# Vision block on one core: the side work between the attention groups in another order

## The chip, the cores and the metric

One core of a Trainium2 chip runs the whole program; the other cores are idle. The metric is the device time of one execution in microseconds (us), as the median of several runs. In the trace PE is TensorE (PEld its weight loads), DVE VectorE, ACT ScalarE, POOL GpSimd, and SP the SyncE, whose only work here is to issue DMAs.

## The reference

```python
x = x + window_attention(layernorm(x))      # x: (16, 56, 56, 32) f32; 7x7 windows shifted by 3, 4 heads of 8
t = x as 16 x 3136 tokens of 32 channels
t = t + moe(layernorm(t))                   # 8 experts of 32x32, each token uses its best 2

# window attention, per window of 49 tokens and head
attn = softmax((q * 8**-0.5) @ k.T)         # no bias inside the softmax
attn = attn + bias[head] + mask[window]     # relative bias and the shift mask are added after it
out  = (attn @ v) joined over heads @ w_proj + b_proj
# moe
p = softmax(x @ router_w + router_b); top 2, renormalised; out = sum of p_k * (x @ expert_w[k] + expert_b[k])
```

## The kernel before

The image batch is cut into 16 units. A unit is one half, 28 columns, of two images: 64 windows, four side by side in the partitions and 16 along. Each unit goes through four phases, and the program is a software pipeline over them: in one step of the main loop the attention of unit u is computed, and between its pieces stand small side tasks of its neighbours. These are the preparation of unit u+1 (`keep`, `xt`, `qk`, `place`, `kmask`, `v`, `ob`), loading and the first layernorm of unit u+2 (`load`, `norm1_*`), projection, second layernorm and router of unit u-1 (`ot`, `y`, `back`, `norm2_*`, `x2t`, `router`, `top2`, `replicate`), and the expert products of unit u-2 (`wt`, `mix`, `mix_drain`, `final`, `store`).

The attention of a unit is four groups g = 0 to 3, of 16 windows each. A group is a chain over all engines, and every link works on the same four PSUM banks `ps_win`: PE writes the unshifted scores (`maximum`, L1232), DVE takes their largest (L907) and splits its negative in two bf16 parts (`ms`, L921 and L923), PE turns these (`shift`, L1240), ACT copies them (`mr`, L801), PE writes the scores again with the shift (`scores`, L1255 and L1261), ACT takes the exponentials (L810), and PE multiplies with the values (`pv`, L1276) while the next `maximum` has to wait until the exponentials have read the banks. I call the DVE maximum of group g `mx0` to `mx3`; the preparation of a unit's own group 0 is done in the step before, so a step runs from one `mx0` to the next.

The side tasks stand in a table, `SIDE_TASKS`, keyed (g, slot): slot 0 after the scores of group g, slot 1 after the next `maximum`, slot 2 after `pv`, slot 3 after `shift`. One function, `macro_step`, walks it in order, and every engine runs through the same list and takes out only what is its own. So the table fixes the order on each engine, and a task moved past tasks of other engines only changes nothing. Engines meet by semaphores. Nothing is scheduled by a planner.

The tasks that matter here, and their engines:

- `top2` 4 (DVE, L1002 to L1004) makes the two probabilities; `top2` 5 to 7 (POOL, L661 to L677, seven instructions in a chain) make the weights in three bf16 parts; `wt` turns them (PE, L1337) and copies them (ACT, L827); each `mix` i spreads them over the partitions in the one bank `ps_weight` (PE, L1348) and DVE multiplies (L1022). With one bank, `mix` i+1 on PE waits for DVE's product of `mix` i.
- `ot` 0 and 1 turn the attention output (PE, L1290) and copy it (ACT, L789); `y` 0 and 1 project it (PE, L1300); `back` 0 and 1 add the input (DVE, L948); `norm2_center` sums (DVE, L897) and subtracts the mean (POOL, L608 and L612).
- `keep` (POOL, L602) copies the loaded input of the next unit; it waits for `back` 1 of the unit two before, whose buffer it takes.
- `final` 0 and 1 turn the expert sum back (PE, L1307) and add (DVE, L1031, `xo`); `ob` 0 and 1 are the bias part of the attention output (PE, L1214).
- `load`, `replicate` and `store` are issued by SP alone; `kmask` is ACT's (L756), `place` POOL's (L636).

Short products share two banks, `ps_shared` and `ps_acc`; `ON_ACC` says which use the second. `bank_free` makes each fill wait for the drain of the one that was in the same bank before it. After the last unit the tasks that remain are interleaved by the counts in `TAIL`.

Of the kernel before, what the change touches and what calls it, by code (L numbers as in the profile page):

```python
# [69 lines left out]
PRE_ORDER = ("keep", "xt", "qk", "place", "kmask", "v", "ob")  # L70
LATE = ("wt", "mix", "mix_drain", "final", "store")
SIDE_TASKS = {
    (0, 0): [("ot", 1), ("keep", 0), ("wt", 0), ("load", 0), ("y", 0), ("mix", 0), ("back", 0), ("mix", 1), ("y", 1), ("back", 1), ("norm2_center", 0), ("xt", 0), ("mix", 2)],
    (0, 1): [("xt", 1), ("mix", 3)],
    (0, 2): [],
    (0, 3): [("norm2_square", 0), ("qk", 0), ("mix", 4)],
    (1, 0): [("mix", 5), ("norm2_scale", 0), ("norm1_center", 0), ("qk", 1), ("mix", 6), ("kmask", 0)],
    (1, 1): [("mix", 7), ("qk", 2)],
    (1, 2): [],
    (1, 3): [("mix", 8)],  # L80
    (2, 0): [("mix", 9), ("mix_drain", 0), ("mix", 10), ("place", 0), ("x2t", 0), ("mix", 11)],
# [1354 lines left out]
```

## Time and profile before

| | us |
|---|---|
| median of 3 runs | 802.82 (799.15 to 818.51) |
| profiled execution, device time | 804.47 |
| its span, first to last instruction | 802.7 |
| mean granted TensorE clock | 0.946 of full speed |
| one step of the main loop at full clock, `mx0` to `mx0` | 44.0 to 44.6 |
| PE / DVE / POOL / ACT busy | 83% / 69% / 64% / 49% |

The device time is 1.8 us above the span. The profiled run lies 1.65 us above the median. The rows below give the start and the duration in us, the engine, the line, the operation, what it writes and reads, and in brackets the idle time before it with what ended it. Durations of PE rows are modelled and overlap a little with the next row. A row of busy time by stretch has the stretch, its length, the busy us (and instructions) of PE, PEld, DVE, ACT and POOL, the granted clock, the DMA share and GB/s; where it is for one line, only that engine's.

### The profile page before, as it was taken

What the parts mean: (1) busy time and instruction counts of PE and PEld (TensorE: products, weight loads), DVE (VectorE), ACT (ScalarE), POOL (GpSimd) and SP (SyncE); (2) the same over time, 40 slices, a digit from 0 to 9 for tenths busy, and PEclk for the clock granted to TensorE, in tenths of its full rate; (3) what the DMA queues carried; (4) which work ended last, traced back from release to release, by engine and by line L of the source; (5) the groups of instructions that cost most, each with busy time, mean ns of one, the idle gap of its engine ahead of it and who ended that gap; (6) DMA issues with size and microseconds to landing.
All of it is one profiled execution on the core that took longest, in us unless ns stands there. A gap on an engine that the chain in (4) does not pass through costs nothing.

```text
span 802.7 us, 29444 instructions
## 1 busy us (share of the span) xinstructions
PE 665.8 (83%) x12602; PEld 439.5 (55%) x12632; DVE 553.3 (69%) x1003; ACT 395.0 (49%) x641; POOL 515.8 (64%) x555
## 2 busy tenths in 40 slices
PE   0678789989798898989898988989898988987775
PEld 0446565656556565656556565656556565655431
DVE  7433567868686868868686667868576777756634
ACT  1555464546474565555463654555464564533100
POOL 4745685859677776859586676859577776442620
PEclk9987998999999999999999899999899999989759
DMA  2000030312304041313113040313203040303140
GB/s 72 21 23 2 22 82 22 84 42 49 69 25 87 24 99 25 84 42 81 44 40 75 13 103 22 83 43 72 52 20 86 22 100 5 83 22 72 31 101 20
DMA packets 16962, 41.48 MB, mean 52 GB/s; under 512 B 9281, under 2 KB 9409, under 8 KB 15297
## 3 DMA queue, kind: packets, MB, share of 16 engines
q1 hardware_dynamic: 16240, 38.59, 21.6%
q8 instruction: 100, 1.64, 0.9%
q10 hardware_dynamic: 592, 1.01, 0.4%
q14 instruction: 30, 0.24, 0.1%
HBM read 7.47 MB, written 6.42 MB: 17 GB/s over the span
## 4 chain that ended last, share of the span: by engine, by line
PE 43%; DVE 36%; issue 8%; POOL 7%; ACT 4%; SPq 0%; DMA 0%; DVEq 0%; POOLq 0%; ACTq 0%
DVE mx L907 9%; PE ps_win L1261 5%; PE ps_weight L1348 4%; PE ps_pv L1276 4%; PE ps_acc L1368 4%; PE ps_win L1232 4%; DVE ms L921 4%; DVE zt L1022 3%; PE ps_shared L1187 3%; DVE x L1022 3%; PE ps_shared L1300 2%; PE ps_win L1255 2%; PE ps_win L1240 2%; DVE ms L923 2%; PE ps_acc L1187 2%
## 5 line engine op out<-in xcount | busy, mean ns | idle before, releaser
L907 DVE TENSOR_REDUCE mx<-ps_win 128x32 f32<-128x1568 f32 x64 | 114.3, 1786 | 36.7 <-PE ps_win L1232 36.7
L1022 DVE TENSOR_TENSOR zt<-ps_weight,x 128x392 f32<-128x392 f32 x118 | 66.1, 561 | 100.3 <-PE ps_weight L1348 100.3
L1276 PEld LDWEIGHTS ps_pv<-vb,pt 128*49 128x49 f32 x4096 | 101.2, 128 | 25.6 <-issue 25.3
L810 ACT ACTIVATE pt<-ps_win 128x1568 f32<-128x1568 f32 x64 | 94.6, 1478 | 41.7 <-PE ps_win L1261 40.3
L1276 PE MATMUL ps_pv<-vb,pt 128*49 128x18 f32 x4096 | 107.4, 200 | 0.0
L1348 PE MATMUL ps_weight<-wt,const_bf_tile 96*128 96x392 bf16 x234 | 81.5, 348 | 20.8 <-DVE zt L1022 19.2
L644 POOL TENSOR_TENSOR on<-on,obs 128x256 f32<-128x256 f32 x64 | 46.6, 729 | 79.0 <-DVE on L934 79.0
L1022 DVE TENSOR_TENSOR x<-ps_weight,x 128x392 f32<-128x392 f32 x116 | 65.3, 563 | 28.7 <-PE ps_weight L1348 27.2
L602 POOL TENSOR_TENSOR x_kept<-xin,weight_tile 112x896 f32<-112x896 f32 x16 | 33.9, 2120 | 68.6 <-DVE x L948 68.6
L590 POOL TENSOR_TENSOR st<-st,minus_half 112x28 f32<-112x28 f32 x16 | 77.0, 4810 | 1.2
L623 POOL TENSOR_TENSOR st<-st,minus_half 112x28 f32<-112x28 f32 x16 | 76.9, 4806 | 1.2
L801 ACT COPY mr<-ps_win 128x512 bf16<-128x512 bf16 x64 | 37.5, 586 | 78.6 <-PE ps_win L1240 76.6
L636 POOL TENSOR_SCALAR qbd<-qp,const_tile 128x392 f32<-128x392 f32 x128 | 75.5, 601 | 0.0
L1261 PE MATMUL ps_win<-qbd,kp 32*49 32x196 f32 x2048 | 74.4, 349 | 0.0
L756 ACT ACTIVATE kbd<-kp,const_tile 128x392 f32<-128x392 f32 x128 | 69.3, 617 | 0.5
L1348 PEld LDWEIGHTS ps_weight<-wt,const_bf_tile 96*128 96x128 bf16 x234 | 23.0, 98 | 80.6 <-DVE zt L1022 39.7
L1232 PE MATMUL ps_win<-kbd,qp 32*49 32x196 f32 x2048 | 60.2, 344 | 5.4 <-ACT pt L810 4.2
L768 ACT COPY vb<-ps_shared 49x512 f32<-49x512 f32 x62 | 36.8, 593 | 40.5 <-PE ps_shared L1198 40.2
L1232 PEld LDWEIGHTS ps_win<-kbd,qp 32*49 32x49 f32 x2048 | 35.2, 122 | 24.9 <-issue 17.4
L1187 PE MATMUL ps_shared<-xt,weight_tile 128*128 128x392 f32 x94 | 44.1, 552 | 0.6 <-ACT xt L734 0.6
L1240 PE MATMUL ps_win<-const_bf_tile,ms 128*128 128x128 bf16 x256 | 26.5, 229 | 21.8 <-DVE ms L923 21.2
L1255 PE MATMUL ps_win<-mr,const_bf_tile 32*49 32x196 bf16 x1024 | 37.1, 267 | 7.2 <-ACT mr L801 7.2
(161 smaller groups left out, 1351.1 us busy)
## 6 DMA issues: line engine op xcount, KB each, us to landing
x<-x SPq DMA_DIRECT2D x48, 392.0 KB, 5.1
x<-x2t SPq DMA_DIRECT2D x64, 98.0 KB, 2.2
xin<-x SPq DMA_DIRECT2D x32, 150.0 KB
out<-xo SPq DMA_DIRECT2D x32, 150.0 KB
xin<-x SPq DMA_DIRECT2D x32, 18.0 KB
out<-xo SPq DMA_DIRECT2D x30, 18.0 KB
xin<-x SPq DMA_DIRECT2D x32, 15.6 KB
xin<-x SPq DMA_DIRECT2D x32, 1.9 KB
```

What stands on the lines that cost most here:

```text
L590: nc.gpsimd.tensor_tensor(st1[:, 4, :], st1[:, 3, :], minus_half[:, :], ALU.pow).then_inc(rstd1, 1)
L623: nc.gpsimd.tensor_tensor(st2[:, 4, :], st2[:, 3, :], minus_half[:, :], ALU.pow).then_inc(rstd2, 1)
L636: nc.gpsimd.tensor_scalar(qbd[i][:, :, h, :], qp[v.par][:, 8 * i:8 * i + 8, :], head_rows[:, h:h + 1], 1.0, ALU.mult, ALU.mult).then_inc(q ...
L756: ins = nc.scalar.activation(kbd[i][:, :, h, :], kp[v.par][:, 8 * i:8 * i + 8, :], ACT.Copy, scale=head_rows[:, h:h + 1])
L810: nc.scalar.activation(pt[g % 2].rearrange("p a x h n -> p a (x h n)"), ps_win[:, :, 0:2 * HN], ACT.Exp).then_inc(probs_ready, 1)
L907: nc.vector.tensor_reduce(mx[g % 2].rearrange("n a x h -> n a (x h)"), ps_win[:, :, 0:8 * N].rearrange("n a (k m) -> n a k m", m=N), AX, A ...
L1022: nc.vector.tensor_tensor(tokens if eh else zt[:, a, :], weight_bank(w, 1 + i)[:, 0:HALF], tokens, ALU.mult).then_inc(weight_drained, 1)
L1187: mm(pre_bank(v, 2 + i)[:, 0:HALF], (wk if i % 2 else wq)[:, :], xt[:, 8 * b:8 * b + 8, :, :].rearrange("p q k i -> p (q k i)"), start=Tru ...
L1232: ins = mm(ps_win[PAD * k:PAD * k + N, a, HN * x:HN * x + HN], qp[u.par][r, q, :], kbd[g // 2][r, q % 8, :, :].rearrange("p h n -> p (h n) ...
L1261: ins = mm(ps_win[PAD * k:PAD * k + N, a, HN * x:HN * x + HN], kp[u.par][r, q, :], qbd[g // 2][r, q % 8, :, :].rearrange("p h n -> p (h n) ...
L1276: ins = mm(ps_pv[PAD * x:PAD * x + N, c0:c0 + SLOT], pt[g % 2][:, a, x, h, :], vb[u.par][:, 2 * g + x, a, h, :], start=True, stop=True)
L1348: mm(weight_bank(w, 1 + i)[:, 0:HALF], weight_sel[:, eh, a, :], wt[:, HALF * half:HALF * half + HALF], start=True, stop=True).then_inc(wei ...
```

## The change

Only the table changes, and one entry of `ON_ACC`. No instruction is added or removed. Two lines of the table and the set:

```diff
-    (0, 0): [("ot", 1), ("keep", 0), ("wt", 0), ("load", 0), ("y", 0), ("mix", 0), ("back", 0), ("mix", 1), ("y", 1), ("back", 1), ("norm2_center", 0), ("xt", 0), ("mix", 2)],
+    (0, 0): [("ot", 1), ("wt", 0), ("keep", 0), ("y", 0), ("back", 0), ("mix", 0), ("y", 1), ("back", 1), ("mix", 1), ("xt", 0), ("norm2_center", 0), ("mix", 2)],
...
-    (3, 2): [("top2", 4), ("mix_drain", 1), ("ob", 0), ("final", 0), ("top2", 5)],
-    (3, 3): [("ot", 0), ("final", 1), ("top2", 6), ("store", 0), ("top2", 7), ("ob", 1)],
+    (3, 2): [("mix_drain", 1)],
+    (3, 3): [("replicate", 0), ("final", 0), ("ob", 0), ("top2", 4), ("top2", 5), ("top2", 6), ("ob", 1), ("final", 1), ("store", 0), ("top2", 7), ("ot", 0)],
...
-ON_ACC = {("ot", 1), ("xt", 1), ("qk", 0), ("y", 1), ("ot", 0), ("ob", 0), ("router", 0), ("x2t", 1)}
+ON_ACC = {("xt", 1), ("qk", 0), ("y", 1), ("ot", 0), ("ob", 0), ("router", 0), ("x2t", 1)}
```

The other moves: `load` from (0, 0) to (0, 3) and `replicate` from (3, 0) to (3, 3); `qk` 1 and `kmask` 0 to the front of (1, 0), with `norm2_scale` ahead of `mix` 5; `place` 0 from (2, 0) to (1, 1); `norm1_square` and `norm1_scale` from (2, 2) and (2, 3) to (2, 1); `place` 1 from (3, 1) to (2, 3); `top2_exp` from (3, 0) to (3, 1).

What becomes of this on PE, from the `pv` of group 3 on (L1276), is this order before:

```order
L1276 MATMUL ps_pv<-vb,pt 49x18 x32
L1214 MATMUL ps_acc<-vb,bt 64x16x16
L1214 MATMUL ps_acc<-vb,bt 64x2x4x16 x2
L1214 MATMUL ps_acc<-vb,bt 64x16x16
L1214 MATMUL ps_acc<-vb,bt 64x2x4x16 x2
L1307 MATMUL ps_weight<-const_tile,ym 112x128 x4
L1240 MATMUL ps_win<-const_bf_tile,ms 128x128 x4
L1290 MATMUL ps_acc<-const_tile,on 128x2x64 x4
L1307 MATMUL ps_weight<-const_tile,ym 112x128 x3
L1214 MATMUL ps_shared<-vb,bt 64x16x16
L1214 MATMUL ps_shared<-vb,bt 64x2x4x16 x2
L1214 MATMUL ps_shared<-vb,bt 64x16x16
```

and this now:

```order
L1276 MATMUL ps_pv<-vb,pt 49x18 x32
L1240 MATMUL ps_win<-const_bf_tile,ms 128x128 x4
L1307 MATMUL ps_weight<-const_tile,ym 112x128 x4
L1214 MATMUL ps_acc<-vb,bt 64x16x16
L1214 MATMUL ps_acc<-vb,bt 64x2x4x16 x2
L1214 MATMUL ps_acc<-vb,bt 64x16x16
L1214 MATMUL ps_acc<-vb,bt 64x2x4x16 x2
L1214 MATMUL ps_shared<-vb,bt 64x16x16
L1214 MATMUL ps_shared<-vb,bt 64x2x4x16 x2
L1214 MATMUL ps_shared<-vb,bt 64x16x16
L1214 MATMUL ps_shared<-vb,bt 64x2x4x16 x2
L1307 MATMUL ps_weight<-const_tile,ym 112x128 x3
```

The turn of the shift (L1240) moves ahead of the first `ob` (the L1214 rows into `ps_acc`) and of `final` 0 (the first L1307), both `ob` stand together, and `ot` 0 (L1290) comes behind `final` 1, as the next row after these twelve.

On DVE, from the normalisation of group 3 (L930, L934) to the sum of the second layernorm (L897), before:

```order
L930 RECIPROCAL rz<-ps_pv 128x32
L934 TENSOR_TENSOR on<-ps_pv,rz 128x16x2x8
L1002 TENSOR_SCALAR top<-top 112x28
L1003 RECIPROCAL top<-top 112x28
L1004 TENSOR_TENSOR top<-top 112x28
L1031 TENSOR_TENSOR xo<-ps_weight,x_1 112x4x4x32
L1031 TENSOR_TENSOR xo<-ps_weight,x_1 112x3x4x32
L1022 TENSOR_TENSOR zt<-ps_weight,x_0 128x392
L948 TENSOR_TENSOR x_1<-ps_shared,x_kept 112x4x4x32
L1022 TENSOR_TENSOR zt<-ps_weight,x_0 128x392
L948 TENSOR_TENSOR x_1<-ps_acc,x_kept 112x3x4x32
L897 TENSOR_REDUCE st<-x_1 112x28
```

and now:

```order
L930 RECIPROCAL rz<-ps_pv 128x32
L934 TENSOR_TENSOR on<-ps_pv,rz 128x16x2x8
L1031 TENSOR_TENSOR xo<-ps_weight,x_1 112x4x4x32
L1002 TENSOR_SCALAR top<-top 112x28
L1003 RECIPROCAL top<-top 112x28
L1004 TENSOR_TENSOR top<-top 112x28
L1031 TENSOR_TENSOR xo<-ps_weight,x_1 112x3x4x32
L948 TENSOR_TENSOR x_1<-ps_shared,x_kept 112x4x4x32
L1022 TENSOR_TENSOR zt<-ps_weight,x_0 128x392
L948 TENSOR_TENSOR x_1<-ps_acc,x_kept 112x3x4x32
L1022 TENSOR_TENSOR zt<-ps_weight,x_0 128x392
L897 TENSOR_REDUCE st<-x_1 112x28
```

`xo` of `final` 0 (L1031) moves ahead of the three instructions of `top2` 4 (L1002 to L1004), and each `back` (L948) ahead of the product (L1022) that stood before it.

On PE in the slot (0, 0), from `ot` 1 (L1290) to `mix` 2 (the last L1348), before:

```order
L1290 MATMUL ps_acc<-const_tile,on 128x2x64 x4
L1337 MATMUL ps_weight<-const_bf_tile,w_parts 96x112 x7
L1300 MATMUL ps_shared<-weight_tile,ot 112x128 x4
L1348 MATMUL ps_weight<-wt,const_bf_tile 128x392 x2
L1300 MATMUL ps_acc<-weight_tile,ot 112x128 x3
L1179 MATMUL ps_shared<-const_tile,xc 128x112 x4
L1348 MATMUL ps_weight<-wt,const_bf_tile 128x392
```

and now:

```order
L1290 MATMUL ps_shared<-const_tile,on 128x2x64 x4
L1337 MATMUL ps_weight<-const_bf_tile,w_parts 96x112 x7
L1300 MATMUL ps_shared<-weight_tile,ot 112x128 x4
L1348 MATMUL ps_weight<-wt,const_bf_tile 128x392
L1300 MATMUL ps_acc<-weight_tile,ot 112x128 x3
L1348 MATMUL ps_weight<-wt,const_bf_tile 128x392
L1179 MATMUL ps_shared<-const_tile,xc 128x112 x4
L1348 MATMUL ps_weight<-wt,const_bf_tile 128x392
```

`mix` 1 (the second L1348) moves behind `y` 1 (the second L1300), and `ot` 1 writes the other bank.

On SP every instruction keeps its place.

## Rows read from the trace of the kernel before

**Rows 1.** The page: the chain that ended last, by engine.

```profile
PE 43%; DVE 36%; issue 8%; POOL 7%; ACT 4%; SPq 0%; DMA 0%; DVEq 0%; POOLq 0%; ACTq 0%
```

**Rows 2.** Busy time by stretch: a full step, and its part mx0 to mx1.

```profile
377.51:421.50 43.99, 38.76 (x776) 25.85 (x779) 33.74 (x62) 24.68 (x40) 32.15 (x35) 1.00 0.26 57
421.50:437.60 16.10, 13.96 (x266) 10.76 (x265) 9.92 (x20) 7.46 (x14) 10.37 (x15) 1.00 0.36 78
```

**Rows 3.** Timeline of DVE, steps of units 9 and 10, mx0 to mx1.

```profile
426.37 0.37 DVE L1004 TENSOR_TENSOR top<-top 112x28 f32<-112x28 f32 x1
...
426.78 0.69 DVE L1031 TENSOR_TENSOR xo<-ps_weight,x 112x512 f32<-112x512 f32 x1
...
434.35 0.68 DVE L948 TENSOR_TENSOR x<-ps_shared,x_kept 112x512 f32<-112x512 f32 x1
...
435.53 0.56 DVE L948 TENSOR_TENSOR x<-ps_acc,x_kept 112x384 f32<-112x384 f32 x1
...
437.60 1.78 DVE L907 TENSOR_REDUCE mx<-ps_win 128x32 f32<-128x1568 f32 x1
...
439.41 1.08 DVE L921 TENSOR_SCALAR ms<-mx 128x32 bf16<-128x32 f32 x1
```

**Rows 4.** Timeline of POOL, the same stretch.

```profile
426.82 0.57 POOL L661 TENSOR_TENSOR pick<-pick,top 112x224 f32<-112x224 f32 x1
...
430.98 0.61 POOL L677 TENSOR_TENSOR w_parts<-mix_rest,w_parts 112x224 bf16<-112x224 f32 x1
...
436.26 2.12 POOL L602 TENSOR_TENSOR x_kept<-xin,weight_tile 112x896 f32<-112x896 f32 x1 [4.67 <-DVE x L948]
...
438.65 1.74 POOL L612 TENSOR_TENSOR xc<-x,st 112x896 f32<-112x896 f32 x1
```

**Rows 5.** Timeline of PE, the same stretch.

```profile
426.40 0.39 PE L1240 MATMUL ps_win<-const_bf_tile,ms 128*128 128x128 bf16 x4
...
427.61 0.51 PE L1307 MATMUL ps_weight<-const_tile,ym 128*112 128x128 f32 x3 [0.24 <-DVE xo L1031]
...
429.31 0.29 PE L1255 MATMUL ps_win<-mr,const_bf_tile 32*49 32x196 bf16 x8
...
431.73 0.52 PE L1337 MATMUL ps_weight<-const_bf_tile,w_parts 112*96 112x112 bf16 x7 [0.65 <-POOL w_parts L677]
...
432.57 1.10 PE L1300 MATMUL ps_shared<-weight_tile,ot 128*112 128x128 f32 x8 [0.32 <-ACT ot L789]
...
433.50 0.33 PE L1348 MATMUL ps_weight<-wt,const_bf_tile 96*128 96x392 bf16 x1
...
440.88 0.61 PE L1240 MATMUL ps_win<-const_bf_tile,ms 128*128 128x128 bf16 x4 [1.23 <-DVE ms L923]
```

**Rows 6.** Timeline of ACT, the same stretch.

```profile
432.30 0.81 ACT L827 COPY wt<-ps_weight 96x784 bf16<-96x784 bf16 x1
```

**Rows 7.** Busy time of L921 alone after mx1, of two units.

```profile
172.00:177.00 5.00, 1.08 (x1) 1.00 0.28 76
710.60:715.60 5.00, 0.24 (x1) 0.75 0.01 3
```

**Rows 8.** Timeline of POOL and of DVE, after mx2 of unit 8.

```profile
401.65 4.80 POOL L623 TENSOR_TENSOR st<-st,minus_half 112x28 f32<-112x28 f32 x1
...
404.43 0.24 DVE L921 TENSOR_SCALAR ms<-mx 128x32 bf16<-128x32 f32 x1
```

**Rows 9.** Busy time by stretch, mx1 to mx2 of units 8, 9 and 10.

```profile
393.39:402.60 9.21, 7.85 (x168) 4.59 (x169) 7.83 (x12) 4.66 (x7) 4.88 (x7) 1.00 0.18 45
437.60:449.48 11.88, 10.51 (x168) 5.46 (x169) 7.92 (x12) 4.75 (x7) 5.52 (x7) 0.71 0.15 37
484.47:495.20 10.73, 9.36 (x168) 5.22 (x169) 7.83 (x12) 4.74 (x7) 4.88 (x7) 0.84 0.15 39
```

**Rows 10.** Timeline of PE after the last unit's attention.

```profile
744.87 0.86 PE L1307 MATMUL ps_weight<-const_tile,ym 128*112 128x128 f32 x3 [0.75 <-DVE xo L1031]
```

**Rows 11.** Timeline of ACT, the same place.

```profile
744.16 0.51 ACT L789 COPY ot<-ps_acc 128x392 f32<-128x392 f32 x1 [3.71 <-PE ps_acc L1290]
```

More of the change, by code:

```diff
@@ L72 @@
 SIDE_TASKS = {
-    (0, 0): [("ot", 1), ("keep", 0), ("wt", 0), ("load", 0), ("y", 0), ("mix", 0), ("back", 0), ("mix", 1), ("y", 1), ("back", 1), ("norm2_center", 0), ("xt", 0), ("mix", 2)],
+    (0, 0): [("ot", 1), ("wt", 0), ("keep", 0), ("y", 0), ("back", 0), ("mix", 0), ("y", 1), ("back", 1), ("mix", 1), ("xt", 0), ("norm2_center", 0), ("mix", 2)],
     (0, 1): [("xt", 1), ("mix", 3)],
     (0, 2): [],
-    (0, 3): [("norm2_square", 0), ("qk", 0), ("mix", 4)],
-    (1, 0): [("mix", 5), ("norm2_scale", 0), ("norm1_center", 0), ("qk", 1), ("mix", 6), ("kmask", 0)],
-    (1, 1): [("mix", 7), ("qk", 2)],
+    (0, 3): [("norm2_square", 0), ("load", 0), ("qk", 0), ("mix", 4)],
+    (1, 0): [("qk", 1), ("kmask", 0), ("norm2_scale", 0), ("mix", 5), ("norm1_center", 0), ("mix", 6)],
+    (1, 1): [("mix", 7), ("qk", 2), ("place", 0)],
     (1, 2): [],
     (1, 3): [("mix", 8)],
-    (2, 0): [("mix", 9), ("mix_drain", 0), ("mix", 10), ("place", 0), ("x2t", 0), ("mix", 11)],
[7 rows of a table removed]
+    (2, 0): [("mix", 9), ("mix_drain", 0), ("mix", 10), ("x2t", 0), ("mix", 11)],
+    (2, 1): [("norm1_square", 0), ("norm1_scale", 0)],
+    (2, 2): [("qk", 3), ("x2t", 1), ("mix", 12)],
+    (2, 3): [("router", 0), ("place", 1), ("kmask", 1), ("top2", 0)],
+    (3, 0): [("mix", 13), ("top2", 1), ("mix", 14), ("top2", 2), ("v", 0), ("mix", 15)],
+    (3, 1): [("top2_exp", 0), ("top2", 3), ("v", 1), ("mix", 16)],
+    (3, 2): [("mix_drain", 1)],
+    (3, 3): [("replicate", 0), ("final", 0), ("ob", 0), ("top2", 4), ("top2", 5), ("top2", 6), ("ob", 1), ("final", 1), ("store", 0), ("top2", 7), ("ot", 0)],
 }
```

5 rows, old and new, of the table SIDE_TASKS are left out of this document.

## The prediction

> **What bounds the kernel now.** I read the page first: no engine is busy for more than 83% of the span, and in the chain that ended last PE has 43% and DVE 36% [rows 1]. So nothing is bound by throughput over the whole; the end is set by a chain that hops between PE and DVE, and what counts is which wait ends last at each hop. Next the stretches: a step at full clock takes 43.99 us, and 16.10 of it lie between mx0 and mx1, where PE is busy 13.96 and DVE 9.92 [rows 2]. The other three parts of a step share the remaining 27.9 us, with the same attention work in each, so mx0 to mx1 is where side work costs most. There I read the timelines of all engines side by side.
>
> Three things are to be seen in it. First, PE is nearly without a gap from `pv` of group 3 until the scores of the next unit's group 0 at 429.31; its one gap is 0.24 us before `final` 1 [rows 5]. Second, after these scores PE waits 0.65 us until POOL has the last of the weight parts (`wt`), then 0.32 us for ACT's copy of `ot` before `y` 0 at 432.57 [rows 5]. Third, mx1 starts at 437.60 and ends at 439.38, but L921 behind it takes 1.08 us and ends at 440.49, and PE waits 1.23 us for it before it turns the shift at 440.88 [rows 3, 5]. Another L921 took 0.24 us [rows 8]. Its end is 0.10 us behind the end of POOL's L612 at 438.65 + 1.74 = 440.39 [rows 4]: DVE has to wait for that POOL instruction. The unit of 172 us has the same 1.08 us, and so have all of units 3 to 14 (1.07 or 1.08, once 1.38); the last unit, which has no `keep` and so an earlier L612, has 0.24 [rows 7]. So the last link before PE in group 1 is not DVE's own work but POOL's chain `back` 1, `keep`, L608, L612.
>
> **Edits that cost nothing.** SP issues `load`, `replicate` and `store` in the same sequence with the same waits, so moving `load` and `replicate` does nothing at all. `kmask` 0 follows `qk` 1 on ACT as before, with `mix` (which is not ACT's) gone from between them; `top2_exp` stays between `v` 0 and `v` 1 on ACT. `wt` and `keep` share no engine. On POOL, `place` 0 (about 2.5 us) now stands before the addition of group 1 and `norm1_scale` (about 7 us) before that of group 2. Who waits for these additions is `ot` 0, some 10 us on; they stay covered. The sum L891 now stands ahead of DVE's normalisation of group 2, 1.07 us, in a run of DVE work whose sum is unchanged, and the square it needs is two us old. `qk` 1 ahead of `mix` 5 leaves PE's sum between scores and maximum unchanged. `norm2_scale` starts about 1.3 us earlier, and its reader `x2t` was not waiting. If that cover were gone, each would cost at most its own length in a step, and I see no such case.
>
> **The turn of the shift ahead of `ob` and `final` 0.** In place of 426.40, PE turns as soon as `pv` is done and the shift is ready, before the 1.3 us of `ob` 0 and most of `final` 0. But the scores stand behind the same PE work (`ob` 0, `ob` 1, `final` 0 and 1, `ot` 0), so they gain only the gap of 0.24 us [rows 5]. That lets `ot` 1 end earlier, and there the next wait takes it all.
>
> **`xo` ahead of `top2` 4.** This is the step that costs. DVE's `xo` takes 0.69 us, and L1004 ended just before it [rows 3]. So L1004 ends 0.69 us later, POOL's chain starts at 427.51 in place of 426.82 and ends at 432.28 in place of 430.98 + 0.61 = 431.59 [rows 4]. PE's `wt` goes from 431.73 to 432.42, ends at 432.94, and `y` 0 follows: 432.57 becomes 432.94, 0.37 later (before, `y` 0 waited for `ot` a further 0.32, which swallows the rest) [rows 5]. ACT's copy goes from 432.30 to 432.99 and ends at 433.80 [rows 6], so `mix` 0 starts at 433.85 in place of 433.50 [rows 5].
>
> **`back` ahead of `mix`.** This gives it back and more. `back` 0 started at 434.35 because it stood behind the product of `mix` 0. Now it starts when `y` 0 is full, 432.94 + 1.10 + 0.05 = 434.09. Then 0.60 for it and 0.48 for the product (start to start): `back` 1 at 435.17 in place of 435.53, 0.36 earlier [rows 3]. `y` 1 is ready by then, since it no longer stands behind `mix` 1. `keep` and L612 follow `back` 1 directly, so L612 ends at 440.03 in place of 440.39 [rows 4], L921 at 440.13, and PE turns at 440.52 in place of 440.88. On DVE itself mx1 comes about 0.1 us later, at 437.7, and ends at 439.5; it has 0.6 us left before it becomes the later of the two. So the step gains 0.36 us, and in groups 1 to 3 nothing behind it changes. Twelve steps, those of units 3 to 14, show the stretched L921: 12 x 0.36 = 4.3 us.
>
> The bounds of this term: at best L921 meets POOL idle and takes 0.24 [rows 7], 0.84 us less, 10 us in all. At worst the early `back` is eaten and the 0.35 us of `mix` 0 reaches mx1 and everything after it, a loss of 4 us in all. I take 4.3 since both ends of it are worked from neighbouring rows of one stretch.
>
> The Trainium skill, page "SBUF — State Buffer", section "Who interferes with whom", says that DVE and GpSimd share a pair of ports as an exclusive lock, held for the whole instruction. L612 and L921 agree with it. The pow of POOL does not: it ran from 401.65 to 406.45, and an L921 inside it at 404.43 took 0.24 us [rows 8]. If the rule held there too, mx2 would already pay some 2 us a step, and an earlier pow would give a part of it back; the row says that there is nothing to give.
>
> **The tail.** `final` 1 now stands before both `ot`, and `ot` 1 of the last unit waits until ACT has copied `ot` 0, 0.51 us [rows 11], where before `final` 1 and its wait of 0.75 us lay between the two [rows 10]. That wait stays, so `ot` 1 comes 0.7 us later on the path. Start-up: nothing.
>
> **Sum.** 804.47 - 4.3 + 0.7 = 800.9 us for the profiled execution, which lies 1.65 above the median: **799 us**, 0.995 of before. A difference under 2% (16 us) is about what a measurement of this kernel cannot tell from none; the three runs of before span more than that.
>
> **Rivals.**
>
> *The falls of the clock go away.* Between mx1 and mx2 unit 8 took 9.21 us at clock 1.00, unit 9 11.88 at 0.71, unit 10 10.73 at 0.84 [rows 9]; units 12 and 13 repeat the pair. Each time the clock fell to 1.2 GHz around the turn of the shift, after the wait of 1.23 us; in the other units the same wait passed without one, so it stands close to the edge. Together 2.7 + 1.5 + 2.8 + 1.5 = 8.5 us. A wait shortened by 0.36 could be on the right side: 799 - 8.5 = 790.5, and 785 with the best end of the term. For it: the wait becomes shorter. Against it: the wait before `wt` becomes longer.
>
> The Trainium skill, page "TensorE: Matmul & The Clock Gate", section "What's actually happening", lets the clock fall by lack of recent activity. The rows agree in kind; what they don't show is how short a wait is short enough.
>
> *The falls multiply: the slower one.* After the scores PE waits 0.65 us for POOL before `wt` now; by the sum above 432.42 - 431.1 = 1.3 us, the longest wait of the step. If it makes the clock fall in each of the twelve steps, at 2.7 us each, in place of the four falls: 32 - 8.5 = 24, or 823 us. It takes two more long falls to use up the gain, and eight to pass 2%. Against it: `wt` and `ot` waits together were 0.97 us before, with no fall there in any unit.
>
> *The gain is eaten.* POOL's chain comes still later, or L612 meets another DVE instruction, and half a microsecond more is lost before `y` 0: 801 to 806. This is also the case that the reordering does nothing on the path.
>
> **Chances.** Forecast (795 to 801) 0.45; falls gone (785 to 794) 0.24; eaten 0.18; falls multiply (806 to 823) 0.13. Half of the second lies beyond 2% faster (under 786.8) with the best end of the term and a few lost falls at the start of the run: 0.13. More than half of the last lies beyond 818.9: 0.08. The range of 8 in 10 leaves out a tenth on each side: 786 to 812.
>
> **What the profile of the changed kernel would show.** L921 after mx1 still above 0.24 us and ending with L612; the turn behind it some 0.4 us earlier after mx0; PE's wait before `wt` at 1.3 us in place of 0.65; `back` 1 ahead of the product of `mix` 1; 43.6 us a step at full clock; `mr` of group 0 over a microsecond earlier without earlier scores. The forecast is wrong if the wait before `wt` exceeds 1.8 us, if a new wait appears on POOL's additions of groups 1 and 2, or if the clock falls in other places or another number than four of the steps.

## The result, and the profile after

The changed kernel takes 831.7 us (median; 826.3 to 838.5), the kernel before 806.3 us in the same comparison. The ratio is 1.036, with a 95% interval of 1.032 to 1.040: clearly slower, where 799 us was forecast. The profiled execution has a span of 828.0 us, 25.3 more than before. Some executions are slow ones with a lower clock: all ratios leave them out, the medians do not, and the profiled executions of e5 and e10 below are of that kind and are read only where the clock is full.

The page barely moves. First the granted clock in 40 slices of the span, in tenths of full speed, then the chain by engine, which answers to [rows 1]:

```profile
PEclk9989999999998989999998989999999999998766
...
PE 42%; DVE 37%; POOL 8%; issue 7%; ACT 5%; DVEq 0%; POOLq 0%; ACTq 0%
```

DVE, POOL and ACT have each a point more of the chain, PE and issue one less. The stretches say where the time went. These are the four parts of one step at full clock (stretch, its us, busy us of PE, PEld, DVE, ACT, POOL, granted clock, DMA share, GB/s):

```profile
392.56:407.89 15.33, 12.21 (x225) 9.39 (x226) 9.17 (x19) 7.10 (x13) 7.37 (x11) 1.00 0.20 46
407.89:416.71 8.82, 8.00 (x171) 4.72 (x170) 7.62 (x12) 5.85 (x9) 5.77 (x7) 1.00 0.19 47
416.71:424.72 8.01, 7.34 (x175) 4.38 (x175) 5.59 (x11) 4.97 (x8) 7.85 (x8) 1.00 0.02 5
424.72:438.12 13.40, 10.77 (x214) 7.58 (x212) 12.44 (x21) 6.58 (x12) 11.27 (x12) 1.00 0.43 92
```

The first part, mx0 to mx1, takes 15.33 us, against 16.10 in [rows 2] and 15.9 in the undisturbed steps; the second takes 8.82 against 9.21 [rows 9]. Both are shorter, as forecast. The last one, mx3 to mx0, takes 13.40 us where it took 10.9 before, and DVE is busy 12.44 us of it with the same 21 instructions as before. That is 2.5 us a step, in the steps of units 2 to 13: 30 us.

Here is the inside of that part: DVE's second run of `top2`, what POOL did meanwhile, and PE behind it.

```profile
433.63 0.38 DVE L969 TENSOR_REDUCE top<-logits 112x28 f32<-112x224 f32 x1
...
434.04 2.37 DVE L970 TENSOR_TENSOR tmp<-logits,top 112x224 f32<-112x224 f32 x1
...
436.45 0.67 DVE L971 TENSOR_TENSOR tmp<-tmp,const_tile 112x224 f32<-112x224 f32 x1
...
437.15 0.46 DVE L996 TENSOR_TENSOR top<-top 112x28 f32<-112x28 f32 x1
...
433.64 1.70 POOL L594 TENSOR_TENSOR xc<-xc,st 112x896 f32<-112x896 f32 x1
...
435.30 0.73 POOL L644 TENSOR_TENSOR on<-on,obs 128x256 f32<-128x256 f32 x1
...
435.98 0.18 POOL L634 TENSOR_TENSOR turn<-minus_half 1x1 f32<-1x1 f32 x1
...
436.16 2.56 POOL L636 TENSOR_SCALAR qbd<-qp,const_tile 128x392 f32<-128x392 f32 x4
...
438.26 0.87 PE L1368 MATMUL ps_acc<-x,weight_tile 128*32 128x392 f32 x8 [1.69 <-DVE x L1022]
...
439.06 2.37 PE L1276 MATMUL ps_pv<-vb,pt 128*49 128x18 f32 x64
```

L970 compares 224 columns and should take 0.39 us. It starts at 434.04 and ends at 436.41. POOL's L594, the scaling at the end of `norm1_scale`, runs from 433.64 to 435.34, and the addition L644 of group 2 follows it without a gap to 436.03; from there to L970's end are 0.38 us, its plain duration. So L970 took as long as if DVE did nothing until both POOL instructions were over, and its own work after that. L971 and L996 are stretched too, to 0.67 and 0.46 us from 0.39 and 0.19, while `place` 1 (L636) runs. DVE shows no idle time: the wait is hidden inside the duration of an instruction. PE then waits 1.69 us for the product behind it, and the `pv` that follows takes 2.37 us in place of the 1.65 us of the other groups: the granted clock fell to 1.2 GHz in it.

Of all executions of that line in the span (min, median, max in ns):

```profile
L970 DVE TENSOR_TENSOR tmp<-logits,top x32: 391/392/2394, 105.5 to 795.4; 112x224 f32<-112x224 f32 x32
```

Before, no L970 took more than 0.41 us. There the last DVE instruction of `top2` in this place, L996, had ended at 420.98 when L594 began:

```profile
420.79 0.19 DVE L996 TENSOR_TENSOR top<-top 112x28 f32<-112x28 f32 x1
...
421.24 1.70 POOL L594 TENSOR_TENSOR xc<-xc,st 112x896 f32<-112x896 f32 x1
```

The two missed each other by 0.26 us here, and by 0.25 to 0.27 us in ten of the twelve steps. In unit 12 it was 0.08 us, and in unit 9 L594 began 0.08 us before L996 was over, without harm. L594 then ran under mx0, a reduction out of PSUM, which took its usual 1.78 us. That was 10.63 us after mx3; now L594 begins 8.92 us after it, since the sum L891, which POOL's chain waits for, starts 2.23 us after mx3 in place of 3.94.

The rest of the profile answers to [rows 3, 5, 10]: PE before `wt`, `y` 0, the turn of group 1 and the last unit's `ot` 1; DVE's `back` 1 and L921 of group 1.

```profile
402.87 0.52 PE L1337 MATMUL ps_weight<-const_bf_tile,w_parts 112*96 112x112 bf16 x7 [2.42 <-POOL w_parts L677]
...
403.23 1.09 PE L1300 MATMUL ps_shared<-weight_tile,ot 128*112 128x128 f32 x8
...
410.77 0.40 PE L1240 MATMUL ps_win<-const_bf_tile,ms 128*128 128x128 bf16 x4 [0.82 <-DVE ms L923]
...
768.77 1.12 PE L1290 MATMUL ps_shared<-const_tile,on 128*128 128x128 f32 x4 [0.60 <-ACT ot L789]
...
405.43 0.55 DVE L948 TENSOR_TENSOR x<-ps_acc,x_kept 112x384 f32<-112x384 f32 x1
...
409.71 0.68 DVE L921 TENSOR_SCALAR ms<-mx 128x32 bf16<-128x32 f32 x1
```

L921 of group 1 takes 0.68 us in place of 1.08, and the turn behind it waits 0.82 us in place of 1.23. The wait before `wt` is 2.42 us in this unit; in units 5, 6, 9 and 10, where PE comes late because its clock is low, it is 0.2 us or less.

In units 7 and 11 there is one more collision, in group 2: POOL's scaling of the second layernorm, L627, starts just ahead of L923 and holds it for 1.80 us in place of 0.30.

```profile
370.63 1.80 DVE L923 SCALAR_TENSOR_TENSOR ms<-mx,ms 128x32 bf16<-128x32 f32 x1
...
370.58 1.70 POOL L627 TENSOR_TENSOR xc<-xc,st 112x896 f32<-112x896 f32 x1
```

### The profile page after: what moved, and what is told of

The parts are those of the page before. It is cut to its first block, busy times and chain, and to the rows that moved or that the text cites. A ratio compares the mean times of both kernels' runs of the same rounds, so it can differ in the third digit from the quotient of the medians.

```text
span 828.0 us, 29457 instructions
## 1 busy us (share of the span) xinstructions
PE 673.6 (81%) x12602; PEld 455.0 (55%) x12632; DVE 570.3 (69%) x1003; ACT 393.7 (48%) x641; POOL 517.5 (63%) x555
## 4 chain that ended last, share of the span: by engine, by line
PE 42%; DVE 37%; POOL 8%; issue 7%; ACT 5%; DVEq 0%; POOLq 0%; ACTq 0%
DVE mx L907 9%; PE ps_pv L1276 5%; PE ps_acc L1368 4%; DVE tmp L970 4%; PE ps_win L1261 4%; PE ps_win L1232 4%; PE ps_shared L1187 3%; PE ps_weight L1348 3%; PE ps_acc L1324 3%; DVE x L1022 3%; DVE ms L921 2%; PE ps_win L1240 2%; DVE zt L1022 2%; PE ps_shared L1300 2%; DVE st L897 2%
## 5 line engine op out<-in xcount | busy, mean ns | idle before, releaser
L1276 PEld LDWEIGHTS ps_pv<-vb,pt 128*49 128x49 f32 x4096 | 105.3, 131 | 25.8 <-issue 25.7
L1276 PE MATMUL ps_pv<-vb,pt 128*49 128x18 f32 x4096 | 111.5, 203 | 0.0
L644 POOL TENSOR_TENSOR on<-on,obs 128x256 f32<-128x256 f32 x64 | 46.5, 727 | 99.0 <-DVE on L934 99.0
L1348 PE MATMUL ps_weight<-wt,const_bf_tile 96*128 96x392 bf16 x234 | 82.0, 351 | 13.3 <-DVE zt L1022 11.6
L1022 DVE TENSOR_TENSOR zt<-ps_weight,x 128x392 f32<-128x392 f32 x118 | 66.1, 560 | 29.8 <-PE ps_weight L1348 29.8
L1022 DVE TENSOR_TENSOR x<-ps_weight,x 128x392 f32<-128x392 f32 x116 | 65.3, 563 | 18.5 <-PE ps_weight L1348 16.9
L636 POOL TENSOR_SCALAR qbd<-qp,const_tile 128x392 f32<-128x392 f32 x128 | 77.4, 618 | 0.0
L1261 PE MATMUL ps_win<-qbd,kp 32*49 32x196 f32 x2048 | 71.8, 338 | 0.0
L1348 PEld LDWEIGHTS ps_weight<-wt,const_bf_tile 96*128 96x128 bf16 x234 | 22.9, 98 | 77.7 <-DVE zt L1022 31.8
L948 DVE TENSOR_TENSOR x<-ps_shared,x_kept 112x512 f32<-112x512 f32 x16 | 11.1, 691 | 78.9 <-PE ps_shared L1300 78.9
L1232 PE MATMUL ps_win<-kbd,qp 32*49 32x196 f32 x2048 | 58.2, 334 | 6.2 <-ACT pt L810 4.9
L1368 PE MATMUL ps_acc<-x,weight_tile 128*32 128x392 f32 x256 | 30.9, 558 | 23.1 <-DVE x L1022 22.9
L1240 PE MATMUL ps_win<-const_bf_tile,ms 128*128 128x128 bf16 x256 | 27.1, 232 | 21.4 <-DVE ms L923 20.4
```

Source lines behind the costliest of these rows:

```text
L636: nc.gpsimd.tensor_scalar(qbd[i][:, :, h, :], qp[v.par][:, 8 * i:8 * i + 8, :], head_rows[:, h:h + 1], 1.0, ALU.mult, ALU.mult).then_inc(q ...
L1022: nc.vector.tensor_tensor(tokens if eh else zt[:, a, :], weight_bank(w, 1 + i)[:, 0:HALF], tokens, ALU.mult).then_inc(weight_drained, 1)
L1232: ins = mm(ps_win[PAD * k:PAD * k + N, a, HN * x:HN * x + HN], qp[u.par][r, q, :], kbd[g // 2][r, q % 8, :, :].rearrange("p h n -> p (h n) ...
L1261: ins = mm(ps_win[PAD * k:PAD * k + N, a, HN * x:HN * x + HN], kp[u.par][r, q, :], qbd[g // 2][r, q % 8, :, :].rearrange("p h n -> p (h n) ...
L1276: ins = mm(ps_pv[PAD * x:PAD * x + N, c0:c0 + SLOT], pt[g % 2][:, a, x, h, :], vb[u.par][:, 2 * g + x, a, h, :], start=True, stop=True)
L1348: mm(weight_bank(w, 1 + i)[:, 0:HALF], weight_sel[:, eh, a, :], wt[:, HALF * half:HALF * half + HALF], start=True, stop=True).then_inc(wei ...
```

## The experiments

Lengths below are between starts of the DVE maximum in the trace, the shortest of units 3 to 13; ratios are against the kernel before on the same chip. The shortest is not always the usual one. From mx1 to mx2 most steps of e1, e3, e4, e5, e7 and e12 take 8.8 us, like the changed kernel; the shorter ones in the table come behind a step in which the clock was low. In e6 mx3 to mx0 is 11.2 us in nine of the eleven steps.

| kernel | us | ratio (95%) | mx0-mx1 | mx1-mx2 | mx2-mx3 | mx3-mx0 |
|---|---|---|---|---|---|---|
| before | 802.8 to 806.6 | 1 | 15.87 | 9.21 | 8.00 | 10.88 |
| changed | 831.7 | 1.036 (1.032 to 1.040) | 15.32 | 8.80 | 7.99 | 13.40 |
| e1 | 808.6 | 1.008 (1.003 to 1.012) | 15.31 | 8.53 | 8.00 | 12.38 |
| e2 | 851.1 | 1.056 (1.047 to 1.065) | 15.37 | 9.21 | 8.00 | 13.42 |
| e3 | 801.6 | 0.999 (0.995 to 1.003) | 16.11 | 8.54 | 8.00 | 10.87 |
| e4 | 802.0 | 0.999 (0.995 to 1.004) | 15.87 | 8.63 | 8.01 | 11.39 |
| e5 | 806.3 | 1.001 (0.998 to 1.005) | 15.32 | 8.65 | 8.00 | 12.38 |
| e6 | 807.8 | 1.003 (1.000 to 1.007) | 15.90 | 9.21 | 8.00 | 10.88 |
| e7 | 803.6 | 0.999 (0.995 to 1.002) | 15.31 | 8.50 | 8.00 | 12.37 |
| e8 | 794.5 | 0.987 (0.984 to 0.991) | 14.74 | 8.79 | 8.00 | 12.37 |
| e9 | 790.2 | 0.984 (0.978 to 0.990) | 15.03 | 9.26 | 8.20 | 10.97 |
| e10 | 825.0 | 1.023 (1.016 to 1.031) | 15.37 | 9.21 | 8.01 | 12.39 |
| e11 | 816.4 | 1.017 (1.010 to 1.023) | 15.53 | 9.60 | 8.19 | 10.97 |
| e12 | 803.4 | 0.996 (0.993 to 1.000) | 15.32 | 8.60 | 8.00 | 11.96 |

**e1: the second half of the first layernorm put back.** Against the changed kernel:

```diff
-    (2, 1): [("norm1_square", 0), ("norm1_scale", 0)],
-    (2, 2): [("qk", 3), ...],
-    (2, 3): [("router", 0), ("place", 1), ...],
+    (2, 1): [],
+    (2, 2): [("norm1_square", 0), ("qk", 3), ...],
+    (2, 3): [("norm1_scale", 0), ("router", 0), ("place", 1), ...],
```

> The changed kernel with one edit undone: norm1_square and norm1_scale stand in (2, 2) and (2, 3) again; all other moves stay. Port theory (POOL's L594 reads two SBUF tiles and holds off DVE's L970, 2.4 us a step): L970 back to 0.39 us, mx3 to mx0 from 13.4 to 10.9 us in 12 steps, 30 us less than the changed kernel and 1 us a step less than before from the other moves, so 790 to 800 us. Place theory (the moves of place 0 and 1 cost the time): place stays moved, so 825 to 835. Clock theory (most of the loss is falls of the clock at PE's longer waits near mx0): L970 may be short, but the time stays over 815.

It took 808.6 us: most of the loss is gone, but not all, and I had expected 790 to 800. L970 is back at 0.39 us, yet mx3 to mx0 is 12.5 us in nearly every step. Two of its DVE rows, and POOL's L594:

```profile
472.22 0.39 DVE L971 TENSOR_TENSOR tmp<-tmp,const_tile 112x224 f32<-112x224 f32 x1
...
472.64 1.82 DVE L996 TENSOR_TENSOR top<-top 112x28 f32<-112x28 f32 x1
...
472.59 1.70 POOL L594 TENSOR_TENSOR xc<-xc,st 112x896 f32<-112x896 f32 x1
```

L594 starts 0.05 us ahead of L996, an instruction on 28 columns, and holds it for its whole length: 1.82 us in place of 0.19. The mechanism is the same; the victim is another.

**e2: the kernel before with this move alone**, the same edit the other way round.

> The kernel before with this one edit alone: norm1_square and norm1_scale moved to (2, 1). Port theory: L970 takes 2.4 us in about 12 steps, 30 us slower than before plus some falls of the clock, 830 to 845 us. Place theory: no change, 800 to 812.

It took 851.1 us, 45 more than before and above the range that I gave. mx3 to mx0 is 13.4 us, 31 us more in the twelve steps; the rest lies ahead of unit 2 and behind unit 13. In nine of the steps L971 is the one that is held, in three L970:

```profile
442.96 2.50 DVE L971 TENSOR_TENSOR tmp<-tmp,const_tile 112x224 f32<-112x224 f32 x1
```

So this one move costs more than the whole change, and the other moves of the change bring some of it back.

**e3: only POOL's order.** `norm1_scale` became two tasks, the sum on DVE early as in the changed kernel, POOL's part behind the addition of group 2. PE, DVE, ACT and SP keep exactly the order of the changed kernel.

```diff
-    (2, 3): [("router", 0), ("place", 1), ...],
+    (2, 3): [("norm1_rescale", 0), ("router", 0), ("place", 1), ...],
...
-                elif step == "norm1_scale":      # in POOL's loop
+                elif step == "norm1_rescale":
                     norm1_scale(unit, i)
...
```

The new name also stands in the list of tasks and, directly behind `norm1_scale`, in the prologue.

> The changed kernel with DVE, ACT, PE and SP in exactly its order; only POOL does its part of norm1_scale (L586 to L594) behind the addition of group 2 again, so L594 starts about 1.5 us later, at the end of the DVE run and under the maximum. Port theory: L970 0.39 us, mx3 to mx0 10.9 us, 790 to 800 us. DVE order theory (the sum L891 ahead of the normalisation of group 2 delays DVE's run or those who wait for it): DVE's order is unchanged, so it stays at 825 to 835.

It took 801.6 us, and the whole loss of the change is gone with no other engine touched. That fells the theory of DVE's order. DVE and POOL of one step:

```profile
377.36 0.39 DVE L970 TENSOR_TENSOR tmp<-logits,top 112x224 f32<-112x224 f32 x1
...
378.22 0.19 DVE L996 TENSOR_TENSOR top<-top 112x28 f32<-112x28 f32 x1
...
380.74 0.72 DVE L921 TENSOR_SCALAR ms<-mx 128x32 bf16<-128x32 f32 x1
...
378.37 1.70 POOL L594 TENSOR_TENSOR xc<-xc,st 112x896 f32<-112x896 f32 x1
```

L594 starts as L996 is nearly over and runs under the maximum; mx3 to mx0 is 10.87 us. But `place` 1 is now later and stands in the way of L921 of group 0, 0.72 us in place of 0.24, and mx0 to mx1 takes 16.1 in place of 15.3 us. That is 0.8 us a step, some 10 us in all. The clock took some more: in nine of the eleven steps of units 3 to 13 it fell to 1.2 GHz around `wt`, where PE had waited 1.96 to 2.44 us, and five of these steps have over 17 us from mx0 to mx1. So it comes out at 0.999 and not at the 790 to 800 that I expected.

**e4: more work.** One small pow more on POOL ahead of L594, from unit 2 on.

```diff
+        pause = [sb(f"pause{i}", [ROWS, 11]) for i in range(4)]
...
+                if v.n >= 2:
+                    nc.gpsimd.tensor_tensor(pause[v.n % 4][:, :], plus_1_c[:, 0:11], minus_half[:, 0:11], ALU.pow)
                 xc = xc1[:, :, :, :].rearrange("p k j c -> p (k j) c")
```

> The changed kernel with work added: from unit 2 on POOL does one more small pow (112x11, about 1.9 us by the 4.8 us of the one of 28 columns) into a spare tile, ahead of L594. Nothing is taken away. Port theory: L594 moves behind L970 and under the maximum, so more work makes the kernel faster, 790 to 802 us; if the small pow itself held DVE off, L970 would stay long and the time at 830 or above. DVE order theory and place theory: 830 to 840.

It took 802.0 us: work added, 30 us gained. In its rows (its lines are numbered three higher here) the first row is L970 and the second L996; the POOL rows are the added pow and then L594:

```profile
421.45 0.66 DVE L973 TENSOR_TENSOR tmp<-logits,top 112x224 f32<-112x224 f32 x1
...
422.83 0.19 DVE L999 TENSOR_TENSOR top<-top 112x28 f32<-112x28 f32 x1
...
421.05 2.11 POOL L595 TENSOR_TENSOR pause<-plus_c,minus_half 112x11 f32<-112x11 f32 x1
...
423.12 1.70 POOL L597 TENSOR_TENSOR xc<-xc,st 112x896 f32<-112x896 f32 x1
```

L594 now comes behind L996. The added pow, which reads eleven columns over 2.1 us, cost L970 and L971 0.27 us each. L923 of group 0 now meets `place` 1 and takes 0.76 us in place of 0.30.

**e12: L594 made small.** From unit 2 on it scales one token column of 28, so the rest of that scaling is left out.

```diff
+                if v.n >= 2:
+                    xc = xc[:, 0:1, :]
+                    nc.gpsimd.tensor_tensor(xc, xc, over(st1[:, 4, 0:1], C), ALU.mult).then_inc(normed1, 1)
+                    return
```

> The changed kernel, in which from unit 2 on POOL's L594 scales one token column (112x32) in place of all 28 (112x896): the rest of the first layernorm's scaling is left out. Nothing else moves; the pow ahead of it and the addition of group 2 behind it stay. If L594's 1.7 us of reading holds DVE off, L970 falls to 0.4 us or, with the addition of 0.7 us now under it, to at most 0.8 and mx3 to mx0 to 10.9 to 11.5 us: 795 to 806 us. If the pow, the addition or DVE's order does it: L970 stays above 1.5 us and the time above 820.

It took 803.4 us, within the first case, though mx3 to mx0 is 11.96, half a microsecond over it. Its DVE lines are numbered four higher: the first rows are L970 and L971. On POOL come L594 (here L596), the addition of group 2 (L648) and `place` 1 (L640):

```profile
422.85 0.77 DVE L974 TENSOR_TENSOR tmp<-logits,top 112x224 f32<-112x224 f32 x1
...
423.65 0.83 DVE L975 TENSOR_TENSOR tmp<-tmp,const_tile 112x224 f32<-112x224 f32 x1
...
422.45 0.24 POOL L596 TENSOR_TENSOR xc<-xc,st 112x32 f32<-112x32 f32 x1
...
422.64 0.73 POOL L648 TENSOR_TENSOR on<-on,obs 128x256 f32<-128x256 f32 x1
...
423.66 2.42 POOL L640 TENSOR_SCALAR qbd<-qp,const_tile 128x392 f32<-128x392 f32 x4
```

L594 takes 0.24 us, and L970 waits only for the addition behind it: it ends 0.25 us after that and takes 0.77 us. L971 and L996 then run beside `place` 1 and take 0.83 and 0.46 us, which with L970 is the 1.1 us over the 10.88 of before. So what holds DVE off is the length of whatever POOL instruction on full tiles is there, not this one's kind; the pow before it, 4.8 us long, runs beside the first L970 of the step, which takes its plain 0.39 us.

**e5 and e6: `place` 0.** e5 is e1 with `place` 0 put back as well, as shown; e6 is the kernel before with `place` 0 alone moved, the same edit the other way round.

```diff
-    (1, 1): [("mix", 7), ("qk", 2), ("place", 0)],
+    (1, 1): [("mix", 7), ("qk", 2)],
-    (2, 0): [("mix", 9), ("mix_drain", 0), ("mix", 10), ("x2t", 0), ("mix", 11)],
+    (2, 0): [("mix", 9), ("mix_drain", 0), ("mix", 10), ("place", 0), ("x2t", 0), ("mix", 11)],
```

> The changed kernel with norm1_square and norm1_scale and also place 0 put back where they were; the moves on PE and of xo, back and mix stay. In e1 DVE's L996 was held for 1.8 us by L594, which started 0.05 us before it. Port theory: with place 0 back POOL holds up L921 of group 3 again, L891 and with it L594 come 0.9 us later, all of the second run of top2 is clear: mx3 to mx0 10.9 us, 798 to 802 us. Theory that L594 isn't the cause and e1's 12.5 us come from the PE reordering: still 12.5 us and 806 to 812.

> The kernel before with place 0 alone moved from (2, 0) to (1, 1). POOL then does it before the addition of group 1, and L921 and L923 of group 3 are free to take 0.24 and 0.30 us. Port theory: a faster L921 makes the kernel slower: L891 and L594 come about 0.9 us earlier, L594 meets L996, mx3 to mx0 12.5 in place of 10.9 us in 12 steps, 822 to 830 us. Theory that place is without effect: 803 to 808.

Both expectations were wrong: 806.3 and 807.8 us. In e5 L921 of group 3 stayed at 0.24 us and mx3 to mx0 at 12.5; in e6 there was no collision with L996 but another. In e6 L921 of group 3 and L996, and on POOL the addition of group 1 and L594:

```profile
466.36 1.03 DVE L921 TENSOR_SCALAR ms<-mx 128x32 bf16<-128x32 f32 x1
...
474.99 0.19 DVE L996 TENSOR_TENSOR top<-top 112x28 f32<-112x28 f32 x1
...
466.57 0.72 POOL L644 TENSOR_TENSOR on<-on,obs 128x256 f32<-128x256 f32 x1
...
475.44 1.70 POOL L594 TENSOR_TENSOR xc<-xc,st 112x896 f32<-112x896 f32 x1
```

With `place` 0 ahead, it is the addition that ends late and holds L921 for 1.03 us, where before it took 0.47 us and L923 0.58; L594 is then late enough. mx3 to mx0 is 0.3 us longer in nine of eleven steps, which is about the 3 us by which e6 is slower. So `place` 0 is not what made POOL early. Something else did, and of the moves that could, I had left only `norm2_scale` ahead of `mix` 5: it lets DVE make the sum L903 without waiting for the product of `mix` 5, and POOL's whole queue moves up.

**e10: the kernel before with that one swap.**

```diff
-    (1, 0): [("mix", 5), ("norm2_scale", 0), ("norm1_center", 0), ("qk", 1), ("mix", 6), ("kmask", 0)],
+    (1, 0): [("norm2_scale", 0), ("mix", 5), ("norm1_center", 0), ("qk", 1), ("mix", 6), ("kmask", 0)],
```

> The kernel before with norm2_scale ahead of mix 5 as the only edit. On PE, ACT, POOL and SP the order is that of before; on DVE two neighbours change places in each step. Port theory: POOL is earlier, L921 of group 3 falls to 0.24 us, L594 starts 0.5 us earlier and meets L996: mx3 to mx0 12.5 in place of 10.9 us, 18 us in all, 818 to 828 us. Without the port: 803 to 808.

It took 825.0 us, 2.3% slower (1.6 to 3.1) and as the port theory said, from two neighbours on DVE that change places. L996, and POOL's L594:

```profile
489.03 1.82 DVE L996 TENSOR_TENSOR top<-top 112x28 f32<-112x28 f32 x1
...
488.97 1.70 POOL L594 TENSOR_TENSOR xc<-xc,st 112x896 f32<-112x896 f32 x1
```

**e7 and e8: the rest of the reordering, step by step.** e7 is e5 with `place` 1 at the end of (3, 3); e8 is e7 with `top2` 4 ahead of `final` 0:

```diff
-    (3, 3): [("replicate", 0), ("final", 0), ("ob", 0), ("top2", 4), ("top2", 5), ..., ("place", 1)],
+    (3, 3): [("replicate", 0), ("top2", 4), ("final", 0), ("ob", 0), ("top2", 5), ..., ("place", 1)],
```

> As e5, and place 1 put to the end of (3, 3), where POOL is idle until keep and DVE too. Port theory: L921 and L923 of group 0 meet no POOL instruction, 0.24 and 0.30 us in place of some 0.5 and 0.6; with the shift turned ahead of ob that reaches the path: mx0 to mx1 15.4 us, a step of 43.1 us in place of 44.2, 788 to 794 us. If PE's work alone sets mx0 to mx1: as e5, 798 to 802.

> As e7, with top2 4 ahead of xo on DVE again, the one edit for which the prediction charged 0.37 to 0.69 us at wt. The order on all other engines is that of e7. If that term was right: wt 0.6 us earlier and the step 0.4 to 0.6 us shorter than in e7, 5 to 7 us less. If the copy of ot is the later one: no change against e7.

e7 took 803.6 us, not 788 to 794: mx0 to mx1 was 15.31 us as expected, but L594 still met L996. It shares e5's wrong premise. e8 took 794.5 us, 9 us less than e7 where 5 to 7 were expected. mx0 to mx1 is 14.74, 0.57 us a step less than in e7 or 7 us in twelve. PE before `wt` in e8:

```profile
385.92 0.52 PE L1337 MATMUL ps_weight<-const_bf_tile,w_parts 112*96 112x112 bf16 x7 [1.46 <-POOL w_parts L677]
```

The wait is 1.46 us in place of 2.40. In e7 the clock fell around `wt` in six of the steps of units 3 to 13, in e8 in none; that this gave the other 2 us is likely and not separated.

**e9: e8 with `norm2_scale` behind `mix` 5 again; e11: e9 with slot (0, 0) in the old order.**

```diff
-    (1, 0): [("qk", 1), ("kmask", 0), ("norm2_scale", 0), ("mix", 5), ("norm1_center", 0), ("mix", 6)],
+    (1, 0): [("qk", 1), ("kmask", 0), ("mix", 5), ("norm2_scale", 0), ("norm1_center", 0), ("mix", 6)],
```

For e11, against e9; of the old order of this slot only `load` and the place of `keep` behind `wt` are then missing:

```diff
-    (0, 0): [("ot", 1), ("wt", 0), ("keep", 0), ("y", 0), ("back", 0), ("mix", 0), ("y", 1), ("back", 1), ("mix", 1), ("xt", 0), ("norm2_center", 0), ("mix", 2)],
+    (0, 0): [("ot", 1), ("wt", 0), ("keep", 0), ("y", 0), ("mix", 0), ("back", 0), ("mix", 1), ("y", 1), ("back", 1), ("norm2_center", 0), ("xt", 0), ("mix", 2)],
```

> As e8, with one swap undone: norm2_scale stands behind mix 5 again. In e8 each step from mx3 to mx0 still takes 12.4 us, with L996 held by L594. Port theory: DVE's sum L903 comes about a microsecond later, POOL's chain with it, place 0 again holds up L921 and L923 of group 3, L891 and L594 come 0.5 us later and L594 starts behind L996: mx3 to mx0 10.9 us, 1.5 us less in 12 steps, 775 to 781 us. Theory that the remaining 1.5 us are PE's new order: 794 as e8.

> As e9, with slot (0, 0) as before the change: back 0 and back 1 behind the products of mix 0 and mix 1, mix 1 ahead of y 1. The prediction gave this edit 0.36 us a step and more against a delay at wt. If right: L921 of group 1 from some 0.7 to 1.1 us, the step 0.4 us longer, 4 to 6 us over e9. If back is covered: as e9.

e9 took 790.2 us, 1.6% below before and the fastest of all; e8 is 1.3% below, and their intervals overlap. mx3 to mx0 went to 10.97 us, because L996 and L594 pass each other again:

```profile
463.93 0.19 DVE L996 TENSOR_TENSOR top<-top 112x28 f32<-112x28 f32 x1
...
464.38 1.70 POOL L594 TENSOR_TENSOR xc<-xc,st 112x896 f32<-112x896 f32 x1
```

It missed the 775 to 781 since the later sum costs elsewhere: mx1 to mx2 is 9.26 against 8.79 us in e8, and mx0 to mx1 15.03 against 14.74. e11 took 816.4 us, 26 us over e9 where 4 to 6 were expected. Its L921 of group 1:

```profile
404.21 1.06 DVE L921 TENSOR_SCALAR ms<-mx 128x32 bf16<-128x32 f32 x1
```

In e9 the same one took 0.65 us. mx0 to mx1 and mx1 to mx2 are longer by 0.50 and 0.34 us, some 10 us in twelve steps, and from unit 2 to unit 14 the trace has 34 us at the low clock against 14 in e9. The expectation had the 0.4 us and not the rest. That the longer wait makes the clock fall more often is argued, not shown.

## Why the prediction was wrong

**The step that failed** stands in "Edits that cost nothing". Of `norm1_scale` ahead of the addition of group 2 the prediction asked only who waits for the addition by a semaphore, found `ot` 0 ten microseconds away, and called it covered; the sum L891 ahead of DVE's normalisation it saw as a run of DVE work with unchanged length. It never asked when POOL's L594 would now run and beside what. The runs showed in its place: L594 begins 1.7 us earlier in the step and, with the addition at its back, holds L970 for 2.0 us in each of twelve steps. e3 shows it without any other change, e4 with work added, e12 by its size. "`norm2_scale` starts about 1.3 us earlier, and its reader `x2t` was not waiting" has the same fault: by e10 that alone costs 19 us. The prediction had found this very kind of wait, L612 on L921, and looked for its effect only where the wait stood already, not where the moved instructions would make a new one.

**A rule that was at hand.** The Trainium skill, page "SBUF — State Buffer", section "Who interferes with whom", has a sentence for it: "A DVE instruction with two SBUF inputs contends with a GpSimd instruction that reads SBUF". L970, L971 and L996 have two SBUF inputs, and the trace agrees with 2.37 and 1.82 us. The prediction drew on the same section of the Trainium skill for the exclusive lock. It found that L612 and L921 agree, saw 0.24 us beside the pow [rows 8], and then asked of the moved tasks only what an earlier pow would do. That reading of the pow was right: in e12 and before, the pow on 28 columns runs beside `top2` instructions, and L970 takes its plain 0.39 us. So that the lock is held for the whole instruction does not fit the pow. The mistake was to carry a result for a POOL instruction on 28 columns over to one on 896.

**The edits that cost nothing, otherwise.** SP's order is unchanged, as said. `place` 0 by itself costs 0.3 us in most steps (e6, 1.003, with an interval that begins at 1.000), by another collision than before and not by a wait for its own length.

**The turn of the shift, and `back` ahead of `mix`.** The forecast was 0.36 us off L921 and the turn; measured, L921 went from 1.08 to 0.68 us and mx1 to mx2 from 9.21 to 8.80, so 0.4 us. e11 agrees: with this slot in its old order L921 is 1.06 us again. mx0 to mx1 gained a further 0.56 us that the sum did not have, and this was POOL's doing as well. Before, `place` 1 ran beside L921 and L923 of group 0, which took 0.45 and 0.59 us in most steps; now `place` 1 is over by then and they take 0.24 and 0.30. e10, with the old order in this slot, has the same short rows and 15.37 us. Both gains together, some 11 us in twelve steps, are in the changed kernel, under the 30 us lost. So the forecast's own term was right in size and cause, and the other gain is one that it had not counted.

**`xo` ahead of `top2` 4.** The sign and the place were right: it costs 0.57 us a step at `wt` (e8 against e7) where the sum had 0.69 at `wt` and 0.37 at `y` 0. The wait before `wt` was 1.96 or 2.42 us in the steps where the clock was full, and not 1.3, since PE arrived earlier than I had it. The prediction gave the scores of group 0 only 0.24 us; in unit 8 they started 6.11 us after mx0, against 7.60 before.

**The tail.** `ot` 1 of the last unit waits 0.60 us for ACT's copy, as forecast, but little of it reaches the end: from unit 14's mx0 to the end it is 152.2 us, against 152.0 before, where the sum had 0.7 more.

**The rivals.** The slower rival was forecast at 823 us, by falls of the clock at the wait before `wt`. That wait did grow to 2.4 us, but most of the time lost was not there: of the stretches of low clock in units 3 to 13, two begin around `wt`, in units 3 and 13. Six begin 1.5 to 1.9 us after mx0, behind PE's 1.7 us wait for DVE, and the other four come later in units 7 and 11, two of them behind the held L923. In the other kernels the rival's falls do appear. Where PE waits some 2 us or more before `wt` in nearly every step (e1, e3, e4, e7, e12), the clock falls around it, from 0.7 us before its start to 1.7 us after, in 5 to 9 of these eleven steps; where it waits 1.5 us or less (before, e2, e6, e8, e9, e11) in none. What makes it fall in one such step and not in the next stays open.

From unit 2 to unit 14 the clock stood at 1.2 GHz for 55 us of the trace, against 27 before, and the steps hold 20 us over their shortest length against 12; some 3 of these 20 are the two held L923. So in the 25 us there are 30 of the held `top2` instructions, about 8 of low clock and L923 together, less 11 to 12 that came back in the steps and 2 ahead of unit 2. The parts are read from one profiled run of each and are good to a few microseconds. That the collision causes the falls behind mx0 is only argued: they are in the changed kernel and in two steps of e2, all behind a wait of 1.7 us, and in e1 and e3, where that wait is 0.8 us or less, there is none; but e3 has 41 us of low clock all the same, nearly all of it from falls at `wt`.

Two of the prediction's own signs of being wrong came true, a wait before `wt` over 1.8 us and falls of the clock in more than four steps. Neither pointed at the place where the time went.

## What to carry to other kernels

When an instruction moves, ask not only who waits for it by a semaphore, but what runs beside it at its new time: between DVE and POOL the neighbours count, and a held instruction showed here as a long duration, not as idle time. Compare the longest and the median duration of each line, and when two long-running queues pass each other by a quarter of a microsecond, step after step, treat that gap as part of the schedule. An earlier start on an engine that is off the path can be a loss.

## What the runs showed of the hardware

- An instruction of DVE that reads two SBUF tiles waits for a running POOL instruction on full tiles to about its end, and for a second one that follows it at once: L970 took 2.37 us behind L594 and L644. The size of the DVE instruction does not matter: L996 on 28 columns, 0.19 us, took 1.82.
- L921 reads one SBUF tile only and is held too: 1.08 us in place of 0.24 beside L612.
- A reduction is not disturbed: out of PSUM, mx0 took 1.78 us with L594 under it; from SBUF, L969 took 0.38 us beside L594.
- POOL's pow on few columns hardly counts: 4.8 us on 28 columns cost L970 nothing, and 2.1 us on 11 columns cost two neighbours 0.27 us each in e4.
- PE's clock fell to 1.2 GHz in other steps with each order. It fell close behind a wait of 0.80 us before the turn in e8 and e9, and stayed full through a wait of 2.42 us before `wt` in units 4, 8 and 12 of the changed kernel, so the length of one wait does not settle it.
